# N-gram sums in 256 columns, the byte product in exact bf16 parts, y copied to SBUF right after its square

## The chip, the cores and the metric

The kernel runs on one core of a Trainium2 chip. A core has five engines that each work through their own list of instructions: PE (TensorE, matmuls and transposes; its weight loads have a row of their own, PEld), DVE (VectorE), ACT (ScalarE), POOL (GpSimd) and SP (SyncE, which only issues DMAs here). They meet through semaphores alone. The metric is the device time of one execution in microseconds (us), the median of three.

## The reference

A small language-model tower over 32 sequences of 512 byte values (16,384 tokens, width H = 128):

```
tokens   enc = [byte_emb[x], mean over n = 3..8 of gate_n * ngram_emb[n][hash of n bytes] / n] @ W_enc.T + b_enc
x3       Y = retention(layernorm(X)) + X                  4 heads of 32, decay mask, causal
         X = gelu(layernorm(Y) @ w1 + b1) @ w2 + b2 + Y
         retention: Q, K (rotated), V; A = Q K^T * decay; y = A V; y normed per head (gn_w, gn_b); swish(G) * yn @ WO
experts  add enc to X, layernorm, logits over 8 experts, top 1, two-layer FFN of that expert, added to the row
```

An n-gram that would reach past the end of its sequence adds nothing. Inputs and outputs are float32.

## The kernel before, in words

`tower_program` (line 133) writes one program per engine. Sequences are taken in 16 **pairs** (`it`); a pair has two sets `s` = 0, 1 (one sequence each) and each set two halves `h` = 0, 1 of 256 tokens (two chunks of 128). So four **streams** (s, h) run side by side, each with two PSUM banks, `bank_a` and `bank_b`. Short names below: s0h1 l1 is set 0, half 1, layer 1.

Every engine's list is made by `main_program` (line 414). Each stream has a main sequence, `attend` then `feed` for three layers (29.8 and 14.4 units), beside it `embed` of the next pair and `route` of the last, and on POOL the gathers. The pieces are generators that `yield` a number, their place in units after the piece's start; `by_progress` (line 385) always takes the piece with the lowest number next. The streams start 0, 11.91, 28.43 and 40.35 units apart (`LAGS`). So hand-written numbers set the order, engine by engine, and it is fixed when the program is built. An engine that reaches an instruction whose semaphore is not there yet stands still, with all that is behind it.

The pieces that matter, each with its semaphore waits:

- `attend`, PE (1164 to 1237): `norm_T` (two transposes of `xn`), projections q, k, v, g (1171), transposes of the rotated q and k (1182), `kv` (1189), scores (1194), values y into `bank_a` (1205), the mean squares (1218, "ms": `sq` times the head matrix into the upper half of `bank_a`), the transposes of the spread rstd into `bank_b` (1224, `rT_y`), and the output projection (1233, "o", tile `zp`).
- The same on ACT (679 to 710): copy and scale of x (`norm_T`), V and tanh of g (685, 686), copies of q, k (689, 691), square of y (696, `sq`), **spread** (701, one rstd per head written over 32 columns, tile `xn<-gr`), and copy of the transposed rstd from PSUM, scaled by `gn_w` (706, tile `zp`).
- On DVE (935 to 989): `xn` (889), rotation (949, 950, 953), swish (957, `sw`), state mask and sum (963, 969), score masks (974), eps onto the mean squares (979, `ms`), **z** (983, 984: y times scaled rstd, plus `gn_b`, times swish; it waits for 706), residual (988).
- On POOL: power -0.5 of the mean squares (611, tile `gr`) and of the norms (584, 599).
- `embed`: 12 gathers of 128 table rows on POOL (573); on DVE the one-hot of the bytes (911) and the weighted sum of the six tables, chunk by chunk (922, 926); on PE two transposes, then per chunk `side_T` times `enc_gram` and `onehot` times `pemb`, all float32 (1159 to 1162); then a norm with moments (894, 897), rstd on POOL in two instructions (590, 591) and the apply (903).
- `route`: the same norm on the last layer's output, small copies into `row` (1013 to 1017), logits, choice, places, and a scatter to DRAM.

After the pairs comes the expert phase (from 2256 us on), which the change leaves alone.

The lines on which the order hangs:

```
LAGS = ((0, 11.91), (28.43, 40.35))
...
            while min(at) < DONE:
                n = at.index(min(at))
                at[n] = next(streams[n], DONE)
...
                yield (24.26, 23.57, 21.54)[l]
                n = CH * HEADS // 2
                act.wait_ge(y_r[s], nth(k, 2, h))
```

Of the kernel before, what the change touches and what calls it, by code (L numbers as in the profile page):

```python
# [8 lines left out]
BF16 = mybir.dt.bfloat16  # L35
# [24 lines left out]
LAGS = ((0, 11.91), (28.43, 40.35))  # L60
TILE = 512
# [12 lines left out]
def columns(widths):  # L74
# [10 lines left out]
    ("before", P), ("gram_scale", NG), ("gram_valid", NG), ("vocab", 1), ("token", CH), ("rank", E),  # L85
# [10 lines left out]
def constants(n_tokens):  # L96
# [24 lines left out]
    c[:, CONST["gram_valid"]] = [[(CH - 1) * P + p + n <= S for n in GRAMS] for p in i]  # L121
    c[:, CONST["gram_row"]] = [k * HASHES for k in range(NG)]
    c[:, CONST["parity"]] = (i[:, None] // HD) % 2 == np.arange(2)[None, :]
    c[:, CONST["vocab"]] = i[:, None]
    c[:, CONST["token"]] = i[:, None] + np.arange(CH)[None, :] * P
# [3 lines left out]
    c[:, CONST["tile"]] = np.arange(64)  # L129
    return c  # L130

def tower_program(nc, x, gram_table, layer_w, params, consts, expert_w, out):
# [10 lines left out]
    with ExitStack() as ctx:  # L144
# [18 lines left out]
        gate = sb("gate", [P, 2, NG])  # L163
# [22 lines left out]
        onehot = two(sb, "onehot", [P, S])  # L186
# [6 lines left out]
        side_mom = two(sb, "side_mom", [P, 2, CH, 2])  # L193
        side_ve = two(sb, "side_ve", [P, CH])
        side_rstd = two(sb, "side_rstd", [P, 2, CH])
# [12 lines left out]
        qkT = two(sb, "qkT", [P, 2, 2, 2, P])  # L208
        qm = two(sb, "qm", [P, 2, HEADS, 2 * P])
        kv = two(sb, "kv", [P, CH - 1, H])  # L210
# [23 lines left out]
        token = two(sb, "token", [P, CH])  # L234
# [17 lines left out]
        mod_i = [lent(qm[0], 0, [NG, P], I32), lent(qm[0], GP, [NG, P], I32), lent(qm[1], 0, [NG, P], I32)]  # L252
        quot_i = lent(qm[1], GP, [NG, P], I32)
# [7 lines left out]
        past = lent(qm[0], 0, [tiles - SETS, E])[0:1]  # L261
        pastn = lent(qm[0], 64 * E, [tiles - SETS, E])[0:1]
# [37 lines left out]
        side_moments = halves("side_norm_moments_ready")  # L300
        side_scale = halves("side_norm_rstd_ready")
        n_ss = halves("norm_square_sums_ready")
        x_s = two(sem, "layer_output_ready")
        x0_s = two(sem, "layer_input_ready")
        x0_ss = two(sem, "layer_input_square_sums_ready")
# [18 lines left out]
        y_ms = two(sem, "y_square_sums_ready")  # L324
        y_r = two(sem, "y_rstd_ready")
        ms_p = two(sem, "y_square_sums_in_psum")
        rT_y = two(sem, "y_rstd_transposed")
        y_rb = two(sem, "y_rstd_spread")
        z_a = two(sem, "y_scale_ready")
# [5 lines left out]
        ff_p = two(sem, "ffn_out_in_psum")  # L335
# [63 lines left out]
        def early(part):  # L399

            for point in part:
                yield APART * point
# [18 lines left out]
        def side_norm(it, k):  # L421

            if k == 0:
                return 2 * it if it else 1
# [949 lines left out]
```

## Time and profile before

| | |
|---|---|
| Time, median of 3 | 2497.04 us (2496.94 to 2498.17) |
| The profiled execution: span of core 0, first to last instruction | 2495.6 us |
| What lies around the span (median less span) | 1.4 us |
| Mean granted clock of TensorE over the span | 0.982 |
| PE, DVE, ACT, POOL busy | 2263.5, 1897.7, 1571.6, 1817.0 us |
| Chain that ended last: PE, DVE, POOL | 61%, 17%, 9% |

The profiled execution is not one of the timed ones; its span is 1.4 us under the median of the timed ones. Times in the views are in us from the span's start, means in ns. "Idle before" is how long the engine had nothing to execute ahead of that instruction, with what ended it.
### The profile page before, as it was taken

How to read it: one execution, taken by the hardware profiler on the slowest of the kernel's cores; microseconds unless marked ns; L12 is line 12 of the kernel's file. 1: busy time of each engine (PE TensorE's matmuls, PEld its weight loads, DVE VectorE, ACT ScalarE, POOL GpSimd, SP SyncE). 2: the span in 40 equal slices, each digit the busy share in tenths (PEclk: the TensorE clock that was granted, in tenths of full speed). 3: DMA queues.
4: the chain of work that ended last, by engine and by line, in shares of the span. 5: the costliest groups of instructions: out<-in, count | busy, mean ns of one | idle time of the engine just before them, and what ended most of it. 6: DMA issues, size and time to landing. Idle time of an engine off the chain costs nothing.

```text
span 2495.6 us, 52521 instructions
## 1 busy us (share of the span) xinstructions
PE 2263.5 (91%) x18256; PEld 1944.6 (78%) x18256; DVE 1897.7 (76%) x6079; ACT 1571.6 (63%) x4925; POOL 1817.0 (73%) x1902
## 2 busy tenths in 40 slices
PE   0389999999999999999999999999999999987874
PEld 0268888888888888888888888888888888875653
DVE  6357888888797978788888788887879797766442
ACT  0157776777767677676767677677676767753431
POOL 4786777777777777777777777777777765345776
PEclk9889999999999999999999999999999999998997
DMA  3722131313131222222221313131311010004653
GB/s 111 278 63 84 24 110 27 111 26 109 28 106 30 71 66 72 65 71 68 68 71 28 109 26 110 28 108 28 110 26 41 26 27 29 3 9 120 168 157 99
DMA packets 107332, 181.47 MB, mean 73 GB/s; under 512 B 23748, under 2 KB 46406, under 8 KB 106960
## 3 DMA queue, kind: packets, MB, share of 16 engines
q1 hardware_dynamic: 73296, 110.87, 13.4%
q0 software_dynamic: 33792, 67.45, 10.2%
q8 instruction: 140, 2.29, 0.4%
q14 instruction: 104, 0.85, 0.1%
HBM read 89.54 MB, written 90.78 MB: 72 GB/s over the span
## 4 chain that ended last, share of the span: by engine, by line
PE 61%; DVE 17%; POOL 9%; issue 6%; ACT 5%; DMA 2%; POOLq 0%; DVEq 0%; SPq 0%
PE psum L1119 52%; PE psum L1138 6%; POOL grams L573 4%; POOL out L638 3%; DVE hid L974 3%; DVE side_n L926 3%; PE psum L1187 2%; ACT hid L724 1%; DVE qk L953 1%; DVE hid L950 1%; DVE qk L949 1%; POOL gr L611 1%; ACT squares L665 1%; ACT qm L691 1%; DVE zp L984 1%
## 5 line engine op out<-in xcount | busy, mean ns | idle before, releaser
L573 POOL DMA_INDIRECT grams<-gram_table,idx_all x768 | 785.2, 1022 | 197.8 <-issue 189.9
L1119 PE MATMUL psum<-xT,lw 128*128 128x256 f32 x1920 | 482.8, 384 | 0.7 <-ACT xT L677 0.7
L1119 PE MATMUL psum<-lw,hid 128*128 128x129 f32 x3072 | 405.7, 277 | 0.9 <-ACT hid L724 0.9
L611 POOL TENSOR_TENSOR gr<-ms,con 128x8 f32<-128x8 f32 x192 | 326.9, 1702 | 105.8 <-DVE ms L979 103.0
L1119 PEld LDWEIGHTS psum<-lw,hid 128*128 128x128 f32 x3072 | 376.9, 192 | 21.0 <-issue 15.6
L584 POOL TENSOR_TENSOR rstd<-ss,con 128x2 f32<-128x2 f32 x320 | 232.4, 729 | 189.5 <-ACT squares L665 185.3
L1119 PEld LDWEIGHTS psum<-xT,lw 128*128 128x128 f32 x1920 | 339.0, 192 | 31.4 <-ACT xT L677 0.9
L724 ACT ACTIVATE hid<-psum,par 128x256 f32<-128x256 f32 x768 | 318.2, 478 | 21.1 <-PE psum L1119 17.6
L677 ACT ACTIVATE xT<-psum,par 128x256 f32<-128x256 f32 x384 | 215.5, 562 | 126.4 <-PE psum L1138 122.7
L1119 PE MATMUL psum<-lw,xT 128*128 128x256 f32 (+1 forms) x1536 | 291.8, 333 | 2.0 <-ACT xT L677 1.5
L1138 PE MATMUL psum<-con,xn 128*128 128x128 f32 x1152 | 239.2, 290 | 43.1 <-DVE xn L889 21.4
L1119 PEld LDWEIGHTS psum<-lw,xT 128*128 128x128 f32 x1536 | 252.0, 194 | 28.7 <-ACT xT L677 6.8
L974 DVE TENSOR_TENSOR hid<-psum,con 128x512 f32<-128x512 f32 x384 | 247.8, 680 | 17.1 <-PE psum L1119 17.0
L1138 PEld LDWEIGHTS psum<-con,xn 128*128 128x128 f32 x1152 | 134.6, 144 | 120.0 <-issue 50.1
L1119 PE MATMUL psum<-qm,qkT 64*128 64x256 f32 x1536 | 215.3, 403 | 12.2 <-DVE kv L963 7.6
L949 DVE TENSOR_TENSOR qk<-psum,con 128x512 f32<-128x512 f32 x192 | 131.8, 686 | 83.1 <-PE psum L1119 82.9
L671 ACT ACTIVATE xn<-Y,rstd 128x128 f32<-128x128 f32 x384 | 132.6, 393 | 79.1 <-POOL rstd L584 77.2
L665 ACT ACTIVATE squares<-Y 128x129 f32<-128x129 f32 x384 | 115.3, 304 | 105.5 <-DVE Y L988 104.4
L926 DVE SCALAR_TENSOR_TENSOR side_n<-grams,gate,side_n 128x128 f32<-128x128 f32 x640 | 181.6, 344 | 0.0
L1119 PEld LDWEIGHTS psum<-qm,qkT 64*128 64x128 f32 x1536 | 135.8, 187 | 51.4 <-issue 23.6
L689 ACT ACTIVATE qkT<-psum 128x512 f32<-128x512 f32 x192 | 115.0, 599 | 85.0 <-PE psum L1187 84.0
L691 ACT ACTIVATE qm<-psum,con 128x256 f32<-128x256 f32 x384 | 160.9, 478 | 0.0
(187 smaller groups left out, 4822.2 us busy)
## 6 DMA issues: line engine op xcount, KB each, us to landing
routed_rows<-pad SPq DMA_DIRECT2D x265, 264.0 KB
grams<-expert_w SPq DMA_DIRECT2D x44, 321.0 KB, 3.0
grams<-gram_table,idx_all POOLq DMA_INDIRECT x768
grams<-routed_rows SPq DMA_DIRECT2D x44, 264.0 KB, 3.1
xb<-x SPq DMA_DIRECT2D x32, 256.0 KB
lw<-layer_w SPq DMA_DIRECT2D x1, 2503.5 KB, 12.1
routed_rows<-row,slot POOLq DMA_INDIRECT x128, 2.4
con<-consts SPq DMA_DIRECT2D x1, 1340.5 KB, 6.1
```

The lines of the kernel that those rows point to most:

```text
L573: pool.indirect_dma_start(grams[s][:, g, c, :], None, gram_table, bass.IndirectOffsetOnAxis(ap=idx_all[:, g, at:at + 1], axis=0))\
L584: pool.tensor_tensor(rstd[s][:, CS[h]], ss[s][:, CS[h]], const("half")[:, 0:2], ALU.pow)\
L611: pool.tensor_tensor(gr[s][:, c], ms[s][:, c], const("half")[:, 0:n], ALU.pow).then_inc(y_r[s], 1)
L665: last = act.activation(scratch[s][:, c, :], src[s][:, c, 1:], ACT.Square, scale=float(H) ** -0.5, accum_out=dst[s][:, c:c + 1])
L677: act.activation(xT[s][:, TS[h]], src[:, 0:2 * P], ACT.Identity, bias=b, scale=w).then_inc(xT_s[s][h], 1)
L691: last = act.activation(qm[s][:, h, j, :], bank_b(s, h)[:, 0:2 * P], ACT.Copy, scale=const("parity")[:, j:j + 1])
L724: last = act.activation(hid[s][:, h, 2 * m + f, :], src[:, f * 2 * P:(f + 1) * 2 * P], ACT.Gelu, bias=param("ffn_b1", l * FB + 2 * m + f))
L926: last = dve.scalar_tensor_tensor(acc[:, c, :], grams[s][:, g, c, :], w, acc[:, c, :], ALU.mult, ALU.add)
L949: dve.tensor_tensor(qk[s][:, cs, :], b.rearrange("p (c n) -> p c n", c=2), cos_v[:, cs, :], ALU.mult)
L974: dve.tensor_tensor(A[s][:, h, m], chunks((a, b)[m]), causal.unsqueeze(1).to_broadcast([P, HEADS, P]), ALU.mult).then_inc(sc_s[s], 1)
L1119: return pe.matmul(dst, lhsT, rhs, start=start, stop=stop)
L1138: last = pe.transpose(dst[:, (c % 2) * P:(c % 2 + 1) * P], src[:, c, :], eye)
```

## The change

1. **Byte product.** `pemb` (byte embedding times encoder, plus bias) is split during setup into three bf16 parts that add up to it exactly. The one-hot becomes bf16 and holds byte b in rows b and b + 64; the first two parts stand in the upper and lower 64 rows of one operand, the third in a second. Per chunk one float32 matmul becomes two bf16 matmuls.
2. **N-gram sums.** The weighted sum takes both chunks at once: six instructions of 256 columns for twelve of 128. N-grams past the end now point at a zero row added to the table (six small instructions in setup) instead of having their own weights.
3. **y.** ACT copies y, scaled by `gn_w`, out of PSUM right behind its square, and signals once for both. The spread rstd is transposed into the upper half of `bank_a`, and z reads it from there: the copy behind the transposes (706) is gone. norm 2 is transposed into `bank_a`. Three waits for `bank_b` move from `rT_y` to the third matmul of w1.
4. **Side norms.** DVE adds eps, POOL has one instruction instead of two. `route` writes moments and token number straight into `row`.
5. **Order.** The numbers move into one table, with the same row for both halves. Those of spread, z, `rT_y` and `ms` are new; the rest stay. `route` of the last pair starts 3 units later.

```
+AT = {
...
+    "dve ms": ((21.5, 20.5, 20), (21.5, 20.5, 20)),
+    "dve z": ((25.5, 24.5, 23.5), (25.5, 24.5, 23.5)),
+    "act spread": ((24, 23, 22), (24, 23, 22)),
+    "pe rT_y": ((25, 24, 23), (25, 24, 23)),
...
-                link(pool.tensor_scalar(side_ve[s][:, CS[h]], side_mom[s][:, k, CS[h], 1], EPS, 1.0, ALU.add, ALU.mult))
-                pool.tensor_tensor(side_rstd[s][:, k, CS[h]], side_ve[s][:, CS[h]], const("half")[:, 0:2], ALU.pow)\
...
+                return pool.tensor_tensor(ap, ap, const("half")[:, 0:2].unsqueeze(2), ALU.pow)
...
-                act.activation(sq[s][:, CS[h], :], chunks(bank_a(s, h))[:, 0:2, :], ACT.Square,
-                               scale=float(HD) ** -0.5).then_inc(y_sq[s], 1)
-                yield (24.26, 23.57, 21.54)[l]
+                act.activation(sq[s][:, CS[h], :], chunks(bank_a(s, h))[:, 0:2, :], ACT.Square)
+                act.activation(zp[s][:, TS[h]], bank_a(s, h)[:, 0:2 * P], ACT.Copy, scale=param("gn_w", l))\
+                   .then_inc(y_sq[s], 1)
+                yield at("act spread", h, l)
...
-                yield (26.38, 25.13, 23.43)[l]
-                act.wait_ge(rT_y[s], nth(k, 2, h))
-                act.activation(zp[s][:, TS[h]], bank_b(s, h)[:, 0:2 * P], ACT.Copy,
-                               scale=param("gn_w", l)).then_inc(z_a[s], 1)
...
+            for k, n in enumerate(GRAMS):
+                ends = hv[:, k, P - n + 1:]
+                last = dve.tensor_scalar(ends, ends, const("beyond"), None, ALU.max)
...
+                for n in range(3):
+                    link(dve.tensor_copy(pemb_part[:, n, :], rest))
+                    if n < 2:
+                        link(dve.tensor_tensor(pemb_rest[:, :], rest, pemb_part[:, n, :], ALU.subtract))
...
+                last.then_inc(s_hash_f, 1)
...
-                    for i, c in enumerate(half_chunks(h)):
-                        w = gate[:, (0, 0, 0, 1)[c], g:g + 1]
...
+                        dve.wait_ge(acc_step[s][h], nth(it, NG, g - 1))
+                        last = dve.scalar_tensor_tensor(acc, grams[s][:, g, CS[h], :], gate[:, g:g + 1], acc,
+                                                        ALU.mult, ALU.add)
...
-                yield (26.94, 26.44, 24.57)[l]
-                dve.wait_ge(z_a[s], nth(k, 2, h))
-                link(dve.tensor_tensor(zp[s][:, ts], a[:, 0:2 * P], zp[s][:, ts], ALU.mult))
+                yield at("dve z", h, l)
+                dve.wait_ge(rT_y[s], nth(k, 2, h))
+                link(dve.tensor_tensor(zp[s][:, ts], a[:, 2 * P:], zp[s][:, ts], ALU.mult))
...
-                    mm(bank_b(s, h)[:, chunk(c % 2)], side_T[s][:, chunk(c)], param("enc_gram"), True, False)
-                    last = mm(bank_b(s, h)[:, chunk(c % 2)], onehot[s][:, chunk(c)], pemb[:, :], False, True)
+                    mm(bank_b(s, h)[:, chunk(c % 2)], side_T[s][:, chunk(c)], param("enc_gram"), c % 2 == 0, False)
+                for c in half_chunks(h):
+                    for n in range(2):
+                        last = mm(bank_b(s, h)[:, chunk(c % 2)], onehot[s][:, chunk(c)], pemb_bf[:, n, :], False, n * (c % 2) == 1)
...
-                half_transposes(b, xn[s], h).then_inc(rT_y[s], 1)
+                half_transposes(a[:, 2 * P:], xn[s], h).then_inc(rT_y[s], 1)
...
-                norm_T(it, s, 2 * l + 1, h, b)
+                norm_T(it, s, 2 * l + 1, h, a)
```

**What it moves: PE.** In the loop over the pairs PE's order is that of before, but for the embed groups. One of them, of before (`side_T` is the transposed n-gram sum):

```order
L1138 MATMUL psum<-con,side_n0 128x128 x2
L1119 MATMUL psum<-par,side_T0 128x128
L1119 MATMUL psum<-pemb,onehot0 128x128
L1119 MATMUL psum<-par,side_T0 128x128
L1119 MATMUL psum<-pemb,onehot0 128x128
L1138 MATMUL psum<-con,xn0 128x128 x2
```

and of the change:

```order
L1192 MATMUL psum<-con,side_n0 128x128 x2
L1172 MATMUL psum<-par,side_T0 128x128 x2
L1172 MATMUL psum<-pemb_bf,onehot0 128x128 x4
L1192 MATMUL psum<-con,xn0 128x128 x2
L1172 MATMUL psum<-con,sq1 128x4 x2
```

Two float32 products with the one-hot became four bf16 ones; nothing else moved.

**ACT, place A**, layer 0 of stream s0h0: its spread (`xn0<-gr0`) against the copies of q and k of s0h1 (`qkT0`, `qm0`). Before:

```order
L665 ACTIVATE squares0_1,ss01<-X01 128x129 x2
L724 ACTIVATE hid1<-psum,par 128x256 x4
L735 ACTIVATE side_T0<-psum 128x256
L689 ACTIVATE qkT0<-psum 128x512
L691 ACTIVATE qm0<-psum,con 128x256 x2
L701 ACTIVATE xn0<-gr0 128x256
L665 ACTIVATE squares1,ss1<-Y11 128x129 x2
L706 ACTIVATE zp0<-psum,par 128x256
```

Changed:

```order
L730 ACTIVATE sq0<-psum 128x256
L731 ACTIVATE zp0<-psum,par 128x256
L699 ACTIVATE squares0_1,ss01<-X01 128x129 x2
L755 ACTIVATE hid1<-psum,par 128x256 x4
L766 ACTIVATE side_T0<-psum 128x256
L736 ACTIVATE xn0<-gr0 128x256
L723 ACTIVATE qkT0<-psum 128x512
L725 ACTIVATE qm0<-psum,con 128x256 x2
L699 ACTIVATE squares1,ss1<-Y11 128x129 x2
```

The spread now stands ahead of the copies of q and k of the other half, and y's copy behind its square.

**DVE, place C**, layer 0 of stream s1h1: its z (`zp1`) against the n-gram sum and the swish (`sw0`) of s0h1 layer 1. Before:

```order
L953 TENSOR_TENSOR qk0<-qk0,hid0 128x512
L979 TENSOR_SCALAR ms0<-psum 128x8
L926 SCALAR_TENSOR_TENSOR side_n0<-grams0,gate,side_n0 128x128 x4
L957 SCALAR_TENSOR_TENSOR sw0<-tg0,psum 128x256
L983 TENSOR_TENSOR zp1<-psum,zp1 128x256
L984 SCALAR_TENSOR_TENSOR zp1<-zp1,par,sw1 128x256
L926 SCALAR_TENSOR_TENSOR side_n0<-grams0,gate,side_n0 128x128 x4
L963 TENSOR_TENSOR kv0<-psum,con 128x128
```

Changed:

```order
L1008 TENSOR_TENSOR qk0<-qk0,hid0 128x512
L1034 TENSOR_SCALAR ms0<-psum 128x8
L1038 TENSOR_TENSOR zp1<-psum,zp1 128x256
L1039 SCALAR_TENSOR_TENSOR zp1<-zp1,par,sw1 128x256
L980 SCALAR_TENSOR_TENSOR side_n0<-grams0,gate,side_n0 128x256 x2
L1012 SCALAR_TENSOR_TENSOR sw0<-tg0,psum 128x256
L980 SCALAR_TENSOR_TENSOR side_n0<-grams0,gate,side_n0 128x256 x2
L1018 TENSOR_TENSOR kv0<-psum,con 128x128
```

z moved ahead of a piece of the n-gram sum and of the swish.

## Rows read from the trace of the kernel before

**Rows 1.** The page: busy time, share of the span and instructions of each engine.
```profile
PE 2263.5 (91%) x18256; PEld 1944.6 (78%) x18256; DVE 1897.7 (76%) x6079; ACT 1571.6 (63%) x4925; POOL 1817.0 (73%) x1902
```

**Rows 2.** 500 us of the pairs: busy PE, PEld, DVE, ACT, POOL; granted clock, DMA.
```profile
1000.00:1500.00 500.00, 490.83 (x4112) 427.71 (x4108) 411.61 (x1318) 351.70 (x1138) 389.29 (x411) 1.00 0.21 63
```

**Rows 3.** Timeline of PE: start, length, line, operation, tiles; idle in brackets.
```profile
1186.08 0.50 PE L1119 MATMUL psum<-con,sq 128*128 128x4 f32 x4
...
1202.24 0.28 PE L1119 MATMUL psum<-bias,three_bf 128*128 128x129 bf16 x2
1202.35 1.11 PE L1119 MATMUL psum<-lw,hid 128*128 128x129 f32 x8
...
1267.17 0.39 PE L1119 MATMUL psum<-pemb,onehot 128*128 128x128 f32 x2
1267.40 0.39 PE L1119 MATMUL psum<-par,side_T 128*128 128x128 f32 x2
...
1272.64 0.44 PE L1138 MATMUL psum<-con,xn 128*128 128x128 f32 x2 [0.71 <-ACT xn L701]
...
1318.08 0.50 PE L1119 MATMUL psum<-con,sq 128*128 128x4 f32 x4
```

**Rows 4.** Place A, timelines of POOL, ACT and PE.
```profile
1186.86 1.67 POOL L611 TENSOR_TENSOR gr<-ms,con 128x8 f32<-128x8 f32 x1 [0.27 <-DVE ms L979]
...
1187.33 0.60 ACT L689 ACTIVATE qkT<-psum 128x512 f32<-128x512 f32 x1
1187.82 0.83 ACT L691 ACTIVATE qm<-psum,con 128x256 f32<-128x256 f32 x2
1188.56 0.41 ACT L701 ACTIVATE xn<-gr 128x256 f32<-128x256 f32 x1
1188.88 0.29 ACT L665 ACTIVATE squares<-Y 128x129 f32<-128x129 f32 x1
...
1189.40 1.13 PE L1119 MATMUL psum<-qm,qkT 64*128 64x256 f32 x8
```

**Rows 5.** Place B, timelines of ACT, DVE and PE.
```profile
1215.26 0.42 ACT L701 ACTIVATE xn<-gr 128x256 f32<-128x256 f32 x1 [0.48 <-POOL gr L611]
...
1216.85 0.42 DVE L957 SCALAR_TENSOR_TENSOR sw<-tg,psum 128x256 f32<-128x256 f32 x1
...
1217.78 0.61 PE L1119 MATMUL psum<-V,qk 128*128 128x128 f32 x4
```

**Rows 6.** Place C, timelines of DVE and PE.
```profile
1228.45 1.13 DVE L926 SCALAR_TENSOR_TENSOR side_n<-grams,gate,side_n 128x128 f32<-128x128 f32 x4
1229.50 0.42 DVE L957 SCALAR_TENSOR_TENSOR sw<-tg,psum 128x256 f32<-128x256 f32 x1
1229.83 0.42 DVE L983 TENSOR_TENSOR zp<-psum,zp 128x256 f32<-128x256 f32 x1
...
1230.69 1.13 DVE L926 SCALAR_TENSOR_TENSOR side_n<-grams,gate,side_n 128x128 f32<-128x128 f32 x4
...
1228.86 0.38 PE L1138 MATMUL psum<-con,xn 128*128 128x128 f32 x2
...
1229.97 0.49 PE L1119 MATMUL psum<-V,qk 128*128 128x128 f32 x2 [0.29 <-DVE sw L957]
```

**Rows 7.** The square and its product, s0h1 layer 1: timelines of ACT and PE.
```profile
1236.33 0.38 ACT L696 ACTIVATE sq<-psum 128x256 f32<-128x256 f32 x1
1236.67 0.56 ACT L677 ACTIVATE xT<-psum,par 128x256 f32<-128x256 f32 x1
...
1236.83 0.59 PE L1119 MATMUL psum<-con,sq 128*128 128x4 f32 x4
```

**Rows 8.** Groups of instructions: line, form, count, busy us, mean ns, idle before.
```profile
L706 ACT ACTIVATE zp<-psum,par 128x256 f32<-128x256 f32 x192 | 92.9, 484 | 26.4 <-PE psum L1138 25.9
...
L926 DVE SCALAR_TENSOR_TENSOR side_n<-grams,gate,side_n 128x128 f32<-128x128 f32 x640 | 181.6, 344 | 0.0
L984 DVE SCALAR_TENSOR_TENSOR zp<-zp,par,sw 128x256 f32<-128x256 f32 x192 | 93.6, 487 | 6.8
```

More of the change, by code:

```diff
@@ L60 @@
 LAGS = ((0, 11.91), (28.43, 40.35))
+EARLY = ((0, 11.91), (28.43, 40.35))
+CLOSING = ((3, 3), (3, 3))
+AT = {
[4 rows of a table added]
+    "act qkT": ((12.27, 11.97, 8.14), (12.27, 11.97, 8.14)),
[8 rows of a table added]
+    "dve rope": ((7.38, 8.39, 6.59), (7.38, 8.39, 6.59)),
[6 rows of a table added]
+    "act spread": ((24, 23, 22), (24, 23, 22)),
+    "pe rT_y": ((25, 24, 23), (25, 24, 23)),
+    "pool gr": ((24.36, 21.76, 21.39), (24.36, 21.76, 21.39)),
+    "pool rstd0": ((53.27,), (53.27,)),
+    "pool rstd": ((68.34,), (68.34,)),
+    "pool rstd_r": ((10.35,), (10.35,)),
[14 rows of a table added]
+    "pool scatter": ((98.01,), (98.01,)),
+    "act accT": ((28.58,), (28.58,)),
+    "act h0": ((46.4,), (46.4,)),
+    "act ss0": ((62.88,), (62.88,)),
+    "act rT": ((23.06,), (23.06,)),
+    "dve onehot": ((2.41,), (2.41,)),
+    "dve acc2": ((4.2,), (4.2,)),
+    "dve acc4": ((5.88,), (5.88,)),
+    "dve mom0": ((49.55,), (49.55,)),
+    "dve x0": ((61.11,), (61.11,)),
+    "dve row": ((2.67,), (2.67,)),
+    "dve rn": ((11.47,), (11.47,)),
+    "dve pick": ((47.84,), (47.84,)),
+    "dve slot": ((61.5,), (61.5,)),
+    "pe accT": ((27.45,), (27.45,)),
+    "pe h0": ((40.24,), (40.24,)),
+    "pe rT": ((21.23,), (21.23,)),
+    "pe logits": ((46.06,), (46.06,)),
+    "pe places": ((59.62,), (59.62,)),
+}
 TILE = 512
@@ L335, in tower_program @@
         ff_p = two(sem, "ffn_out_in_psum")
+        r_mom = two(sem, "router_moments_ready")
+        r_scale = two(sem, "router_rstd_ready")
         r_n = two(sem, "router_norm_applied")
@@ L397, in sequences, with early @@
                     yield feed(it, s, l, h), FEED
-        def early(part):
+        def early(part, after=0):
             for point in part:
-                yield APART * point
+                yield after + APART * point
         def beside(s, h, embed, route):
-            yield early(embed(0, s, h)), FIRST + ROUTE
+            yield early(embed(0, s, h)), FIRST + ROUTE + LAGS[s][h] - EARLY[s][h]
             for it in range(pairs):
@@ L411, in beside @@
                 else:
-                    yield early(route(it, s, h)), 0
+                    yield early(route(it, s, h), CLOSING[s][h]), 0
         def main_program(embed, attend, feed, route, *others):
@@ L417, in main_program, with at @@
             by_progress(*[one_by_one(lag + FIRST, *sequences(s, h, attend, feed)) for s, h, lag in streams],
-                        *[one_by_one(lag, *beside(s, h, embed, route)) for s, h, lag in streams],
-                        *[one_by_one(lag, *other(s, h)) for s, h, lag in streams for other in others])
-        def side_norm(it, k):
-            if k == 0:
-                return 2 * it if it else 1
-            return (2 * it + 3 if it + 1 < pairs else 2 * it + 2)
+                        *[one_by_one(EARLY[s][h], *beside(s, h, embed, route)) for s, h, _ in streams],
+                        *[one_by_one(EARLY[s][h], *other(s, h)) for s, h, _ in streams for other in others])
+        def at(name, h, l=0):
+            return AT[name][h][l]
         def pads_done(group):
@@ L1000, in route @@
                 cs = CS[h]
-                yield 2.67
+                moments = row[s][:, :, H + 1:H + 3]
+                yield at("dve row", h)
                 if it:
@@ L1004, in route @@
                 dve.wait_ge(x_s[s], nth(it * LAYERS + LAYERS - 1, 2, h))
+                token = row[s][:, cs, H:H + 1].bitcast(I32)
+                dve.tensor_scalar(token, token, float(2 * S), None, ALU.add)
                 for c in half_chunks(h):
```

262 lines of the change are left out of this document (135 added, 127 removed), and 30 rows, old and new, of the table AT.

## The prediction

> **What bounds it now.** I read the page first. PE is busy 91% of the span, the others 63 to 76% [rows 1]. Then the busy time by stretch: in 500 us of the pairs PE works 490.8 us at the full granted clock (1.00, the 2.4 GHz level), DVE 411.6, POOL 389.3 and ACT 351.7 [rows 2]. So PE's list is the clockwork of the kernel. But "busy" hides small stops: a product that comes 0.1 us late is covered in this view by the modelled tail of the one before it. So I went on to the timeline, and it repeats. The product with the squares of s0h0 layer 0 starts at 1186.08 and at 1318.08 us [rows 3], which makes a **period** of 132.0 us for a pair. The 16 pairs are one start and some 15 such periods. Whatever the change does in one period counts 15 times. I made the sum for one period, against this execution (span 2495.6), and add the result to the median, which is 1.4 us more.
>
> PE stops in a period only where its next piece waits for a chain over other engines. The longest such stop with its own idle entry is the transposes of the spread rstd of s1h1 layer 1, 0.71 us after ACT [rows 3]. Another is `kv` of s0h1 layer 1, which waits for the swish on DVE [rows 6]. Everything else fits with a few tenths to spare, and the order numbers make it fit. The question for a change like this is less what it saves than which instruction comes to stand in front of which.
>
> **Part 1, the byte product: minus 0.9 us a period.** A float32 product with the one-hot takes 0.23 us (1267.17 to 1267.40) [rows 3], for two instructions. Two bf16 products of 129 columns take 0.11 us (1202.24 to 1202.35) [rows 3]. A group of two chunks goes from 2 x 0.23 to 4 x 0.055 = 0.22 us, saves 0.23 to 0.24, and a period has four groups: 0.92 us, over 64 groups **14.7 us**. The measured pair is of the same kind (weights of 128 columns in bf16, product behind product), so I take its price. The Trainium skill (TensorE: Matmul & The Clock Gate, Back-to-back issue gap) speaks against that: it gives about 81 ns for a sustained matmul of 128 columns with its weight load. By that page a group would save 0.46 - 0.32 = 0.14 us, 9 us in all. The trace does not agree for a pair of such products (55 ns each), and it has no four in a row.
>
> Not all of it is kept. Two of the four groups stand between the start of a chain and a stop that waits for it: the group at 1267 lies ahead of the 0.71 us stop at 1272.64 [rows 3]. There PE only comes earlier to the same wait. I keep half, **0.45 us**; bounds 0 and 0.92.
>
> **Part 2, sums of 256 columns: DVE 0 to -1.5 us a period, PE -0.2.** The 128-column step costs 0.284 us (181.6 us over 640) [rows 8]. A 256-column one lasts 0.487 (z's second) [rows 8] and now waits for its predecessor, some 0.035 us more (6.8 us idle over 192). Two steps at 0.57 become one at 0.52: 0.05 us on five steps and four groups, 1 us of DVE. With the larger first step I say 1.5. Side norms and `route` trade small instructions of DVE about evenly, and POOL loses eight short ones in a period. DVE's other 80% hides this. Where a PE stop waits for DVE's queue it helps by a tenth or two: I take 0.2 us for all.
>
> **Part 3, y copied early.** The copy costs ACT 0.484 us before and after [rows 8]; the removed step was copy, plus two semaphore hops, between `rT_y` and z. So z may start some 0.5 us earlier. Before that, the squares' product now waits for square and copy. At s0h1 layer 1 the square starts at 1236.33, ACT could take the copy at 1236.67, it ends 0.48 later at 1237.15, and the product, which started 0.12 us after the square's end, starts at 1237.27 instead of 1236.83 [rows 7]: plus 0.44. There are twelve such places in a period, so the bounds are 0 and 5.3 us. Most have slack; I expect four to be touched, three of them partly hidden by a stop that follows or by a chain that z's earlier start shortens. I take **0.3 us**, near the one place that is sure. The moved waits for `bank_b` cost nothing: what they wait for was done microseconds before, and they now come later.
>
> **Part 4, the order.** This decides. On PE nothing moved, but ACT and DVE execute what comes next or stand still.
>
> *Place A, +0.9 us.* POOL's power for s0h0 ends at 1186.86 + 1.67 = 1188.53. Before, ACT used that time for the q and k copies of s0h1 (1187.33 to 1188.65) and did the spread at 1188.56. Now the spread stands ahead of them. It can't start sooner, so ACT waits 1.2 us, and the copies start at 1188.56 + 0.32 = 1188.88 and end 1.32 us later, 1190.20. PE's scores of s0h1 started at 1189.40 [rows 4]. They need these copies, so they start at 1190.3: 0.9 us late. Behind them on PE stand the second half of w2 of s1h0 and all the rest. The bounds are 0.8, if a wake-up costs nothing, and 1.0.
>
> *Place B, +0.4 us.* The same for s1h0 layer 0. The spread, which waits for POOL until 1215.26 in either order, now has q and k of s1h1 behind it, and V and tanh of s0h0 behind those; V moves from 1215.58 to 1215.26 + 0.32 + 1.23 = 1216.8. Tanh ends at 1217.5, and z (0.86 us, see C) also has been put ahead of the swish on DVE. The swish goes from 1216.85 to 1217.7 and ends at 1218.1; `kv` on PE stood at 1217.78 [rows 5] and starts at 1218.2.
>
> *Place C, +1.3 us.* z of s1h1 layer 0 stood behind a piece of the n-gram sum and the swish of s0h1. It now stands ahead of both, at 1228.45. But its transposes run on PE at 1228.86 and end at 1229.24, and their place on PE is the same. DVE idles 0.8 us, does z (0.86 us, from 1229.83 to 1230.69), then the piece of the sum (1.05 us before, 1.0 now), and comes to the swish at 1229.28 + 0.86 + 1.0 = 1231.1 instead of 1229.50. `kv` of s0h1 already waited for the swish at 1229.97 [rows 6], so all of it reaches PE: +1.6 us. The scores behind it had waited some 0.3 us for DVE, which is now covered: 1.3 net. Bounds: 1.0 and 1.6.
>
> *Elsewhere*: z of s0h1 layer 1 stands ahead of a rotation, an `ms` of layer 2 behind a piece of the sum, and z of s0h0 layer 2 ahead of a residual. Each moves a chain by 0.7 to 1 us (one z, 0.86 us, or one piece of the sum, 1.05) [rows 6] that has some slack. I take **0.5 us** for all; the bounds are 0 and 2.6, three times z.
>
> **The sum of a period**: 0.9 + 0.4 + 1.3 + 0.5 + 0.3 - 0.45 - 0.2 = 2.75 us. These were worked out one by one, while a stop early in the period gives the later chains slack. So I take 0.4 off: **2.35 us**, 15 times **35 us**. The start adds, as an estimate, 1 us for six small instructions ahead of the gather indices (a tenth or two each, well under the 0.41 us of a 256-column step [rows 6]) and 1.5 for place A, where ACT waits for a POOL busy with gathers; the end, a single chain, gains about 1 by z's shorter path and the lighter norms. In all +36: 2497 + 36 = **2533 us**. A measurement can tell about 0.2% (5 us) from no change.
>
> **The rivals.** *PE's work is what counts* (faster): PE is 98% busy in the pairs [rows 2], so what is taken from it comes off the end and the new waits fall into slack. For it: PE's share, and z's chain is 0.5 us shorter. The Trainium skill says so as well (Perfetto Trace Analysis, Identifying Performance Opportunities: improve the most-contended engine). Against it: places A and C, where an engine is made to wait for something that cannot be there. It gives -14.7, 2482 us. Chance 0.13.
>
> *Only the early copy costs* (same): the order works out, but the squares' product waits 0.44 us at two places in a period: +13 us against -14.7. 2495 us, chance 0.07.
>
> *Every wait adds up* (slower still): nothing is absorbed, the saving is all lost at the stops. Then the sum is 3.4, and with twice the allowance for the places elsewhere 3.9 us, +58 or so: 2558 us. Chance 0.12.
>
> *The forecast*: chance 0.68. Its own range is 1.2 to 3.5 us a period, 2515 to 2550. That the queues hold strictly is its condition. The skill says they do (TensorE: Matmul & The Clock Gate, the table at its head: strict FIFO on ACT, DVE and POOL). ACT's 0.48 us of idle ahead of the spread, with V of another half ready behind it [rows 5], agrees.
>
> **Range and chances.** From 2502, which leaves out the two quick cases, to 2555, which takes in most of the slow one. Faster 0.13, same 0.07, slower 0.80.
>
> **What would show it.** In the profile after: a period of 134 to 135 us; four bf16 products in 0.22 us in the embed groups; DVE idle some 0.8 us ahead of the z of s1h1 layer 0, released by PE; ACT idle over 1 us ahead of the spread of s0h0 layer 0, with the q and k copies behind it; more idle on PE for ACT's q and k copies and for the swish. PE's share should fall to about 89%. I am wrong if the period is 131 to 132 us, or if it is longer while ACT and DVE never wait at A and C.

## The result, and the profile after

| | before | changed |
|---|---|---|
| Time, median of 4 runs each | 2496.99 us (2496.45 to 2498.17) | 2575.97 us (2573.95 to 2577.18) |
| Ratio | | 1.0315, 95% interval 1.0300 to 1.0329 |
| Span of the profiled execution | 2495.6 us | 2574.3 us |

Slower by 79 us. The forecast was plus 36 (2533 us), its range ended at 2555 and the slowest rival stood at 2558. The sign was right, the size less than half.

The page of the changed kernel, busy time of each engine, for [rows 1]; then 500 us of the pairs, for [rows 2]:

```profile
PE 2284.7 (89%) x18258; PEld 1942.4 (75%) x18258; DVE 1880.7 (73%) x5582; ACT 1555.8 (60%) x4925; POOL 1767.6 (69%) x1774
```

```profile
1000.00:1500.00 500.00, 478.55 (x3974) 412.91 (x3973) 396.62 (x1169) 337.55 (x1104) 365.03 (x367) 1.00 0.21 67
```

In 500 us every engine is busy for less time: PE 478.6 us for 490.8. No engine became fuller; what grew is the time in which they wait for each other. The chain that ended last was 61% PE before, and is now:

```profile
PE 47%; DVE 22%; POOL 15%; issue 9%; ACT 6%; DMA 1%; POOLq 0%; SPq 0%; DVEq 0%
```

PE's timeline over one period, changed kernel, for [rows 3] to [rows 7] (read in short windows, so that a group can show fewer products than it has):

```profile
1173.62 0.39 PE L1172 MATMUL psum<-pemb_bf,onehot 128*128 128x128 bf16 x4
1173.84 0.39 PE L1192 MATMUL psum<-con,xn 128*128 128x128 f32 x2
...
1224.35 0.39 PE L1172 MATMUL psum<-con,sq 128*128 128x4 f32 x3
...
1228.73 0.49 PE L1172 MATMUL psum<-qm,qkT 64*128 64x256 f32 x2 [0.78 <-ACT qm L725]
...
1257.75 0.49 PE L1172 MATMUL psum<-V,qk 128*128 128x128 f32 x2 [0.23 <-DVE sw L1012]
...
1271.61 0.49 PE L1172 MATMUL psum<-V,qk 128*128 128x128 f32 x2 [1.85 <-DVE sw L1012]
...
1279.08 0.38 PE L1172 MATMUL psum<-con,sq 128*128 128x4 f32 x2 [0.67 <-ACT zp L731]
...
1287.73 0.44 PE L1243 MATMUL psum<-con,qk 128*128 128x128 f32 x2 [0.23 <-DVE qk L1008]
...
1315.34 0.33 PE L1243 MATMUL psum<-con,qk 128*128 128x128 f32 x1 [0.36 <-DVE qk L1008]
...
1360.42 0.39 PE L1172 MATMUL psum<-con,sq 128*128 128x4 f32 x3
```

From one product with the squares of s0h0 layer 0 to the next it is 136.07 us, for 132.0. Each named place has its row: A at 1228.73, B at 1257.75, C at 1271.61, the early copy at 1279.08. The idle entry is a little under what PE loses, since the modelled tail of the last product covers some 0.2 us. Measured from start to start against the same pieces without a wait, A went from 0.15 to 1.00 us, B from 0 to 0.39, the `kv` of C from 0.45 to 2.01.

What the queues look like there, first ACT at place A, then DVE at place C:

```profile
1227.04 0.41 ACT L736 ACTIVATE xn<-gr 128x256 f32<-128x256 f32 x1 [1.38 <-POOL gr L645]
1227.36 0.58 ACT L723 ACTIVATE qkT<-psum 128x512 f32<-128x512 f32 x1
```

```profile
1269.36 0.42 DVE L1038 TENSOR_TENSOR zp<-psum,zp 128x256 f32<-128x256 f32 x1 [0.89 <-PE psum L1192]
1269.82 0.48 DVE L1039 SCALAR_TENSOR_TENSOR zp<-zp,par,sw 128x256 f32<-128x256 f32 x1
1270.22 1.00 DVE L980 SCALAR_TENSOR_TENSOR side_n<-grams,gate,side_n 128x256 f32<-128x256 f32 x2
1271.14 0.41 DVE L1012 SCALAR_TENSOR_TENSOR sw<-tg,psum 128x256 f32<-128x256 f32 x1
```

ACT stands 1.38 us for POOL with the q and k copies ready behind it. DVE stands 0.89 us for the transposes, then does z and the sum piece, and the swish on which PE waits comes last. Both are as the prediction drew them.

The view of waits sums such idle time over the whole span (engine, line, what it waited for: us, times, longest). Of PE's rows the ones that bear on the change, before and then changed:

```profile
PE psum L1138 <- ACT xn L701: 18.5, 33, 2.5
PE psum L1119 <- ACT qm L691: 3.3, 7, 1.2
PE psum L1119 <- DVE sw L957: 3.1, 11, 0.3
PE psum L1119 <- ACT sq L696: 1.8, 3, 0.8
```

```profile
PE psum L1172 <- DVE sw L1012: 32.4, 32, 1.9
PE psum L1172 <- ACT zp L731: 15.6, 33, 1.1
PE psum L1172 <- ACT qm L725: 13.4, 17, 1.2
PE psum L1192 <- ACT xn L736: 12.6, 25, 2.5
PE psum L1243 <- DVE qk L1008: 7.4, 26, 0.6
```

Larger rows, such as one wait of 37.0 us before and 38.0 now, lie in the main in setup and the expert phase and differ by at most 3.4 us.

Two things the prediction did not have. The swish and the square with its copy now stand first among the waits of the pairs, the second with 33 waits, two in a period. And the periods are not alike: of the fourteen behind the first (from the first projection of s0h0 in one pair to that in the next), nine are 135.7 to 136.1 us and five 137.4 to 138.0. In those five TensorE's clock falls right behind place C. Windows of 3.4 us (columns as in [rows 2], the granted clock third from the end), four of the five, and the same place in an ordinary period:

```profile
724.70:728.10 3.40, 3.40 (x18) 2.98 (x18) 1.38 (x5) 0.51 (x2) 0.68 (x1) 0.50 0.19 43
997.80:1001.20 3.40, 3.40 (x16) 3.08 (x15) 1.12 (x4) 0.81 (x3) 0.96 (x1) 0.50 0.14 39
1543.90:1547.30 3.40, 3.40 (x18) 3.07 (x17) 1.12 (x4) 0.81 (x3) 0.96 (x1) 0.50 0.17 43
1953.50:1956.90 3.40, 3.40 (x18) 3.07 (x18) 1.14 (x5) 0.70 (x2) 0.95 (x1) 0.50 0.15 39
1271.90:1275.30 3.40, 3.40 (x29) 2.86 (x29) 2.60 (x8) 1.01 (x4) 0.96 (x1) 1.00 0.13 39
```

At 0.50, the 1.2 GHz level, PE gets 16 to 18 instructions through where 29 fit at 1.00. It was full in all of them; what came before was the stop of 1.85 us, which ended 0.2 to 0.6 us before the clock fell. That stop is as long in the nine periods where the clock stays. The kernel before has no such stretch between 160 and 2230 us.

### The profile page after: what moved, and what is told of

It reads as the page before. It is cut to its first block, busy times and chain, and to the rows that moved or that the text cites. A ratio compares the mean times of both kernels' runs of the same rounds, so it can differ in the third digit from the quotient of the medians.

```text
span 2574.3 us, 51781 instructions
## 1 busy us (share of the span) xinstructions
PE 2284.7 (89%) x18258; PEld 1942.4 (75%) x18258; DVE 1880.7 (73%) x5582; ACT 1555.8 (60%) x4925; POOL 1767.6 (69%) x1774
## 4 chain that ended last, share of the span: by engine, by line
PE 47%; DVE 22%; POOL 15%; issue 9%; ACT 6%; DMA 1%; POOLq 0%; SPq 0%; DVEq 0%
PE psum L1172 41%; POOL grams L610 5%; PE psum L1192 4%; POOL out L672 3%; DVE hid L1029 3%; POOL gr L645 3%; DVE qk L1008 2%; POOL rstd L621 2%; ACT squares L699 2%; DVE qk L1004 2%; DVE hid L1005 2%; PE psum L1243 2%; DVE zp L1039 2%; DVE zp L1038 2%; DVE side_n L980 2%
## 5 line engine op out<-in xcount | busy, mean ns | idle before, releaser
L610 POOL DMA_INDIRECT grams<-gram_table,idx_all x768 | 769.8, 1002 | 198.9 <-issue 190.1
L1172 PE MATMUL psum<-qm,qkT 64*128 64x256 f32 x1536 | 216.1, 404 | 21.6 <-ACT qm L725 13.4
L736 ACT ACTIVATE xn<-gr 128x256 f32<-128x256 f32 x192 | 81.0, 422 | 158.5 <-POOL gr L645 158.1
```

The costliest lines, as they stand in the source:

```text
L610: pool.indirect_dma_start(grams[s][:, g, c, :], None, gram_table, bass.IndirectOffsetOnAxis(ap=idx_all[:, g, at:at + 1], axis=0))\
L1172: return pe.matmul(dst, lhsT, rhs, start=start, stop=stop)
```

## The experiments

The theory after the comparison: the new order numbers cost most (places A, B, C and waits behind them, and the clock behind C). The rival: the early copy holds up the squares' product and all else follows.

**One set of four, the kernel before at 2496.5 us beside them.** First the order numbers of before on the otherwise changed kernel:

```diff
-    "dve ms": ((21.5, 20.5, 20), ...      "dve z": ((25.5, 24.5, 23.5), ...
+    "dve ms": ((21.32, 21.92, 19.52), ... "dve z": ((26.94, 26.44, 24.57), ...
-    "act spread": ((24, 23, 22), ...      "pe rT_y": ((25, 24, 23), ...
+    "act spread": ((24.26, 23.57, 21.54), ... "pe rT_y": ((25.36, 23.79, 22.97), ...
```

> The change with the four order rows of the kernel before (ms, z, spread, transposes of the rstd); everything else of the change stays, the early copy of y too. Theory 1, the order: places A, B and C cost 0.85 + 0.39 + 1.34 = 2.6 us a period by the stops of PE in the two traces, two waits for the copies of q and k another 0.9, and the stretches at half clock some 9 us in all; 15 x 3.5 + 9 = 61 us go, 2515 us are left. Theory 2, the early copy is what costs (the product with the squares waits, and all else follows from the late chain): then 30 us or more stay above the kernel before, 2540 us or more. In both the squares' product still waits, 1.4 us a period.

Measured 2502.09 us, ratio to before 1.0022 (1.0012 to 1.0031). Undoing the order numbers takes back 74 of the 79 us. The rival is out. The estimate of 61 was too small: an ordinary period got 3.9 us shorter and not 3.5, mainly because the squares' product of s0h1 layer 1 now waits 0.3 us where it waited 0.8; the first pair gave 5.4 us, and the end 3.8, which the estimate did not have.

Then z's number alone:

```diff
-    "dve z": ((25.5, 24.5, 23.5), (25.5, 24.5, 23.5)),
+    "dve z": ((26.94, 26.44, 24.57), (26.94, 26.44, 24.57)),
```

> The change with z's order row alone put back. Theory 1: place C goes (1.34 us a period net), a wait for the rotated q and k with it (0.4), and every stretch at half clock in the middle of the pairs (some 9 us), while A and B stay: 2576 - 15 x 1.75 - 9 = 2541 us. Rival, the early copy holds z's chain back anyway: z is late wherever it stands, less than 15 us go, 2561 us or more. Rival on the clock: it falls for another reason than the stop at place C, then the half-clock stretches stay and 2550 is left.

Measured 2527.89 us, ratio 1.0129 (1.0112 to 1.0146): 48 us for z. And place B is gone: `kv` of s0h0 layer 1 follows its predecessor without a stop, although the spread still stands ahead of V. The waits for the q and k copies grew instead:

```profile
PE psum L1172 <- ACT qm L725: 29.7, 33, 1.2
PE psum L1192 <- ACT xn L736: 10.4, 22, 1.7
PE psum L1172 <- ACT zp L731: 7.7, 33, 0.9
```

29.7 us for 13.4, and 33 times for 17: once the swish is no longer late, the scores of s0h1 layer 1 wait for the copies that stand behind the spread. Place C had hidden that.

Then the old y path on top of the old numbers: the square signals by itself, the copy waits for the transposes in the other bank.

```diff
-                act.activation(zp[s][:, TS[h]], bank_a(s, h)[:, 0:2 * P], ACT.Copy, scale=param("gn_w", l))\
-                   .then_inc(y_sq[s], 1)
...
+                yield (26.38, 25.13, 23.43)[l]
+                act.wait_ge(rT_y[s], nth(k, 2, h))
+                act.activation(zp[s][:, TS[h]], bank_b(s, h)[:, 0:2 * P], ACT.Copy, scale=param("gn_w", l))\
+                   .then_inc(z_a[s], 1)
```

> As e1_old_numbers, and also part 3 undone: the square signals by itself, y's scaled rstd is copied behind the transposes, which go to the other bank again. What is left of the change is the bf16 byte product, the 256-column sums and the lighter norms. Theory 1 and the prediction's terms: 0.65 us a period under the kernel before, 2487 us; the difference to e1_old_numbers is then the true price of the early copy, 28 us, where the waits of the squares' product alone would make 1.4 x 15 = 21 and the prediction's term 5. Rival, the early copy pays for itself by z's shorter chain: within 8 us of e1_old_numbers.

Measured 2488.61 us, ratio 0.9968 (0.9957 to 0.9978). The early copy, with the move between banks that goes with it, costs 13.5 us under the old order, 0.9 a period. It lies between the two figures expected, and well above the prediction's 0.3. The row of s0h1 layer 1 with the early copy and old order, and without it:

```profile
1239.20 0.61 PE L1172 MATMUL psum<-con,sq 128*128 128x4 f32 x4 [0.15 <-ACT zp L731]
```

```profile
1229.34 0.59 PE L1175 MATMUL psum<-con,sq 128*128 128x4 f32 x4
```

Last the kernel before with the bf16 byte product and nothing else:

```diff
-                    last = mm(bank_b(s, h)[:, chunk(c % 2)], onehot[s][:, chunk(c)], pemb[:, :], False, True)
+                for c in half_chunks(h):
+                    for n in range(2):
+                        last = mm(bank_b(s, h)[:, chunk(c % 2)], onehot[s][:, chunk(c)], pemb_bf[:, n, :], False, n * (c % 2) == 1)
```

> The kernel before with the byte product in bf16 parts and nothing else. Prediction: half of 0.92 us a period is kept, 2490 us. Rival, PE's work is what counts: 14.7 us, 2482 us. Rival, nothing is kept since the stops behind take it all: 2497 us. If four bf16 products in a row cost 81 ns each and not 55, a group saves 0.14 us and the whole 9 at the most: 2488 us or more, and the starts of the products in the trace are 0.32 us apart over a group instead of 0.22.

Measured 2488.76 us, ratio 0.9971 (0.9959 to 0.9984): 7.7 us, half of the 14.7. Its trace has the four in a row, 0.23 us from start to start of what follows:

```profile
1131.45 0.39 PE L1137 MATMUL psum<-pemb_bf,onehot 128*128 128x128 bf16 x4
1131.68 0.39 PE L1157 MATMUL psum<-con,xn 128*128 128x128 f32 x2
```

The stop at s1h1 layer 1, ACT's spread ahead of the transposes, has the size it had (0.96 us from start to start in both; `ACT xn` costs PE 18.9 us in it, for 18.5 before). Had the group ahead of it only brought PE sooner to the same wait, it would be 0.23 us longer, so the other half does not go there. The traces have it at other places: 0.12 us at the squares' product of s1h1 layer 1, 0.18 at the transposes right ahead of that of s0h1 layer 2, which wait for `xn` of DVE, and 0.05 at each of two more products.

**A second set of four, before at 2496.4 us.** z's number for place C alone:

```diff
-    "dve z": ((25.5, 24.5, 23.5), (25.5, 24.5, 23.5)),
+    "dve z": ((25.5, 24.5, 23.5), (26.94, 24.5, 23.5)),
```

> The change with z's order number of layer 0 put back for the second halves (h = 1) alone: place C, where z stands ahead of a piece of the n-gram sum and of the swish, and one spot in s0h1. Theory 1, with the stop of 1.85 us that makes the clock fall: 1.3 us a period and the 3.4 us stretches at half clock among the pairs go (9 us), 2576 - 20 - 9 = 2547 us. Rival on the clock: the stretches come from PE's idle share as a whole and stay, 2556 us. Rival on the place: z of layers 1 and 2 carries most of the 48 us that z's three numbers brought, then 2560 us or more are left.

Measured 2541.08 us, ratio 1.0179 (1.0162 to 1.0196). One entry of the table is worth 35 us. The clock is 1.00 from 160 to 2230 us, with no stretch below, where the changed kernel has 0.99. This kernel, then the changed one:

```profile
160.00:2230.00 2070.00, 1995.68 (x16597) 1723.67 (x16600) 1645.53 (x4837) 1414.15 (x4612) 1468.13 (x1476) 1.00 0.19 58
```

```profile
160.00:2230.00 2070.00, 1976.31 (x16321) 1704.99 (x16322) 1623.38 (x4760) 1389.91 (x4534) 1458.98 (x1465) 0.99 0.19 58
```

The period is 134.6 us, 1.4 less than an ordinary one of the change: from start to start `kv` of s0h1 loses 1.8 us less and the squares' product behind it 0.5 less, but the scores 1.1 more, for the q and k copies. The slow periods that are gone bring 8.5 us, the first pair 5.9.

The spread's numbers alone:

```diff
-    "act spread": ((24, 23, 22), (24, 23, 22)),
+    "act spread": ((24.26, 23.57, 21.54), (24.26, 23.57, 21.54)),
```

> The change with the spread's three order numbers put back (ACT's order but for the y copies as before): places A and B go (0.85 + 0.39), and the wait for q and k of s0h1 layer 2 that stayed with z's old numbers (0.5); the stop ahead of the transposes of s1h1 layer 1 comes back (0.5). Theory 1: 2576 - 15 x 1.2 = 2557 us. Rival: place C holds the period anyway, and what is won at A and B is lost there: within 5 us of the change.

Measured 2558.43 us, ratio 1.0250 (1.0232 to 1.0267), 17.5 us. PE's timeline at A, B and C, and at s0h1 layer 2:

```profile
1218.33 1.13 PE L1172 MATMUL psum<-qm,qkT 64*128 64x256 f32 x8
...
1247.36 0.71 PE L1172 MATMUL psum<-V,qk 128*128 128x128 f32 x4 [0.23 <-DVE sw L1012]
...
1261.21 0.49 PE L1172 MATMUL psum<-V,qk 128*128 128x128 f32 x2 [1.85 <-DVE sw L1012]
...
1305.69 0.44 PE L1192 MATMUL psum<-con,xn 128*128 128x128 f32 x2 [0.71 <-ACT xn L736]
1305.96 0.60 PE L1243 MATMUL psum<-con,qk 128*128 128x128 f32 x4
```

A is gone. **B is not**: with ACT's order as before it is as large as ever, so it is z ahead of the swish that makes it, not the spread. The wait at 1315.34 of the change is gone too, and the 0.71 us stop of before is back. C is there, and with it the stretches at 0.50, in six of the fourteen periods here. With z's new number the spread's costs 17.5 us; with z's old one it costs, together with `ms` and `rT_y`, 2527.9 - 2502.1 = 26 us, since C no longer hides the late q and k copies.

The number of `ms` alone:

> The change with the order numbers of ms (eps onto the mean squares) alone put back. Theory 1: it moves one small instruction of DVE in s1 layer 1 and layer 2, worth a few tenths at the most, 2570 to 2577 us. Rival: the late ms of layer 1, behind z, is part of the chain that ends in the wait for the rotated q and k, then 6 us or more go.

Measured 2576.86 us, ratio 1.0323 (1.0305 to 1.0340): nothing. The ordinary period grew to 136.5 us and there were two slow ones for five, although PE stops 1.92 us at C in every period.

A version that might keep z's shorter chain and lose the stop: y is copied right behind the spread, while PE transposes the spread into the other bank.

```diff
                    .then_inc(y_rb[s], 1)
+                act.activation(zp[s][:, TS[h]], bank_a(s, h)[:, 0:2 * P], ACT.Copy, scale=param("gn_w", l))\
+                   .then_inc(z_a[s], 1)
```

> As e5_old_y (order and banks of before, light norms, 256-column sums, bf16 product), but y is copied on ACT right behind the spread, while PE transposes the spread into the other bank; the square signals by itself. Keeps z's shorter chain without the wait of the squares' product. Expected if the mechanism is right: no stop at the squares' product, those at the output projection gone, 2484 us (2480 to 2488) against 2488.6. Rival: 0.48 us of copy behind the spread comes ahead of V, tanh or the q and k copies of another stream and costs at each of two or three such places what it takes there: 2495 us or more.

Measured 2488.65 us, ratio 0.9969 (0.9957 to 0.9982), the same as with the old y path. The shorter chain of z brings nothing under the old order, where 2484 us was expected: the stops that end with z are few there, and the copy behind the spread makes the scores of s0h1 layer 1 wait 0.3 us longer for the q and k copies (0.92 us from start to start for 0.61), which was the rival. Both beat the kernel before by 0.3%, and both leave out of the change what cost.

**Sets that say less.** The next ten runs came on chips where the kernel before took 2635, 2634 and 2596 us. There engines stop for 2 us and more with no releaser in the trace (shown as "remote"), as in these rows of the waits of e14_spread_s1h1 (DVE, then ACT), which no trace of the two sets above has:

```profile
DVE X L1055 <- remote: 29.5, 15, 2.2
```

```profile
ACT xT L712 <- remote: 33.7, 14, 3.3
```

Only ratios within a set can be read. Place C by itself, on the old numbers:

```diff
-    "dve z": ((26.94, 26.44, 24.57), (26.94, 26.44, 24.57)),
+    "dve z": ((26.94, 26.44, 24.57), (25.8, 26.44, 24.57)),
```

> As e1_old_numbers, with place C alone made as in the change: z of s1h1 layer 0 behind the ms and ahead of the piece of the n-gram sum and the swish. The prediction's term, 1.3 us a period, 20 us, gives 2522 us; if the stop of PE is again 1.85 us and the clock falls behind it in a third of the periods, 8 us more, 2530 us. Rival on the clock: it falls only with the change's other stops as well, 2522 us and no stretch at half clock among the pairs. Rival on additivity: with z's other places as before the period absorbs half of it, 2512 us.

> The kernel of e15_place_c_alone a third time. Where the kernel before takes 2497 us: 2522 us by the prediction's 1.3 us a period, 2530 us with the clock falling behind the stop in a third of the periods, 2512 us if half is absorbed. Where it takes 2635 us again: 21 us above it, as in the two sets so far.

It ran three times, in one set of each chip (e15_place_c_alone, r15_place_c, q15_place_c): 2658.85, 2655.67 and 2618.34 us, ratios 1.0073 (1.0045 to 1.0100), 1.0082 (1.0065 to 1.0099) and 1.0087 (1.0061 to 1.0114). With 1.0022 for the same kernel without it, C alone costs 0.5 to 0.65%, 13 to 16 us, if the ratios carry over; the prediction's term would be 20. The traces say more. PE stops 1.80 to 1.85 us at C in nearly every period of all three, and the scores behind it come 0.35 us sooner than without the edit: some 1.45 us a period at the place itself, 22 us in all, with A, B and the rest as in the old order. Whether the period absorbs the rest of it or the other stops of these chips cover it stays open. In q15_place_c the clock falls behind C in three of the fourteen periods and nowhere else among them, so the change's other stops are not needed for that.

The early copy in the new order, copied behind the spread instead:

> The change with all its new order numbers, but y is copied behind the spread instead of behind the square, the square signals by itself, and the transposes of the rstd go to the other bank. Theory: the stops of the squares' product (1.4 us a period in the change) are the copy's alone and go, 2576 - 20 = 2556 us. Rival: half of them are a late y by the new order (in e9_old_spread one of them moved from 0.79 to 0.60 us with nothing but ACT's order), then 2564 us. Second rival: with the spread ahead of V and of the q and k copies, 0.48 us of copy behind it costs there what it frees, within 5 us of the change.

> The kernel of e12_copy_behind_new_order a third time. Where the kernel before takes 2497 us: 2556 us if the stops of the squares' product are the copy's alone, 2564 us if half of them are the new order's, 2571 us or more if the copy behind the spread costs what it frees. Where it takes 2635 us again: 63 us above it.

Three times as well (e12_copy_behind_new_order, r12_copy_behind, q12_copy_behind), 2698.86, 2696.55 and 2673.6 us, ratios 1.0245 (1.0213 to 1.0277), 1.0247 (1.0220 to 1.0274) and 1.0294 (1.0270 to 1.0318); the change stood at 1.0315 elsewhere. Between 5 and 17 us better, and not settled. The traces show what is gained and lost. Two of the change's three stops of the squares' product (s0h1 layer 0, s1h1 layer 1) are gone; at s0h1 layer 1 some 0.3 to 0.4 us of 0.81 stay without any copy ahead, so that part is the new order's. The scores at place A start 0.36 us later than in the change, since the copy now stands ahead of those of q and k.

Place A alone:

> The change with the spread's order number of layer 0 put back for the first halves alone: place A, and the spread's part of place B. The prediction's term for A: 0.85 us a period at the scores of s0h1 layer 0 go, 13 us, and with place C's 1.85 us stop still there the half-clock stretches stay: 2563 us. In e9_old_spread the stop of place B stayed with the spread's old numbers, so the spread has no part in it and nothing more is expected here. Rival: place C is fed by the same chain and takes back what A gives, 2572 us or more.

Twice (e13_spread_one_place, r13_spread), 2680.5 and 2674.79 us, ratios 1.0156 (1.0129 to 1.0184) and 1.0142 (1.0124 to 1.0159), 40 us better than the change on the other chips where 13 were expected. The changed kernel itself did not run on these chips, so this isn't a price of place A. In both traces the scores of s0h1 layer 0 start 0.20 us behind their predecessor, for 1.05 in the change, and the stop at C is still 1.8 us: C took nothing back.

The one order number of the change that helps (the spread of s1h1 layer 1 ahead of V):

> As e5_old_y, with one order number moved by 0.13: the spread of s1h1 layer 1 stands ahead of V and tanh of s0h1, where the power of POOL is ready 0.3 us after V began. What may be better than both kernels: the 0.85 us stop ahead of the transposes shrinks to the 0.27 that it has in the change, 0.58 us a period, 2488.6 - 9 = 2480 us. Rival: PE comes earlier to the next wait, or V and tanh 0.6 us later make one, 2486 us or more.

Twice (e14_spread_s1h1, r14_spread_s1h1), 2633.44 and 2628.5 us, ratios 0.9990 (0.9971 to 1.0008) and 0.9985 (0.9970 to 1.0000): no gain over the 0.9968 of the kernel that it was built on can be seen. The stop did shrink in e14_spread_s1h1, from 0.85 to a mean of 0.34 us from start to start; `kv` of s0h1 layer 1, behind the later V and tanh, lost 0.83 us for a mean of 0.10 in e5_old_y, as the rival had it, though part of that may be the chip's.

Not tried: the square signalling by itself while the copy stays right behind it. PE would write the bank that ACT reads, and what that does no run here shows.

## Why the prediction was wrong, and where it was right

The forecast was plus 36 us and the kernel got 79 slower. Its signs held: PE's share fell to 89%, DVE stood 0.89 us ahead of z, ACT 1.38 ahead of the spread. The period was to be 134 to 135 us and was 136.07.

**Part 1, right in both numbers, wrong in where the half goes.** 0.055 us for a bf16 product, also with four in a row. By the Trainium skill's 81 ns (TensorE: Matmul & The Clock Gate, Back-to-back issue gap) a group would last 0.32 us; it lasts 0.22 to 0.23, so the trace disagrees. Half was kept (0.49 us a period in e6_bf16_only for 0.45), but not for the reason given: the 0.71 us stop did not take it. Taking half was luck.

**Part 2, right.** The old-path kernel has a period of 131.2 us where the bf16 product alone has 131.5: 0.2 to 0.3 us, with the lighter norms in it. The medians are equal all the same (2488.61 and 2488.76), since its end is 5.5 us longer.

**Part 3, mis-sized: 0.3 us forecast, 0.9 measured alone, some 1.4 of stops in the change.** The step that failed is "I expect four to be touched, three of them partly hidden", with its value of 0.3. Four were touched: with the old order the squares' product loses 0.24, 0.30, 0.37 and 0.23 us against e5_old_y (s0h1 layers 0 and 1, s1h1 layer 1, s0h1 layer 2), and of these 1.14 us the period shows 0.9. In the change the fourth is hidden behind another stop, and the other three lose 0.24, 0.81 and 0.37. The 0.81 are not the copy's alone, since the square itself comes later there in the new order. One sure place was taken as the value, although the sum of like places was what had to be bounded; "most have slack" was said and not read off for the other eleven.

**Place A, right**: 0.85 us for 0.9, by ACT's queue as drawn.

**Place B, right in size (0.39 for 0.4), wrong in cause.** The step gave the delay to both, V and tanh 1.2 us later behind the spread and z ahead of the swish. The spread's old numbers leave B, z's old ones take it away. V came later and had the slack.

**Place C, right for the stop, without its effect on the clock.** `kv` lost 1.56 us more, its scores 0.2 less: 1.36 net against 1.3. Not in the sum: the clock. The prediction put that at nothing, without a reason. The stop of 1.85 us was followed by 3.4 us at half clock in five periods, 8.5 us in all (137.6, 137.4, 138.0, 137.8 and 137.7 against 136.0). Without the stop (z's number back at C alone, or all of z's) there is none. On these chips the stop is needed for it and isn't enough: the same stop brought it in five of fourteen periods in the change, in six with the spread's old numbers and in two with the `ms` number.

**Elsewhere, 0.5 forecast.** The q and k transposes of s1h0 layer 1, behind a rotation that waited for z, cost 0.39 and were on the list. Those of s0h1 layer 2 cost 0.49, and weren't: that is the spread, which the prediction looked at for layer 0 alone. `ms` was on the list and costs nothing. Half a dozen of 0.1 to 0.33 us, the largest at an embed group of s1h1, are in the main paid for by two gains: the stop of 1272.64 [rows 3] lost 0.59 us less, a `places` product 0.35.

**The discount of 0.4, wrong.** The period absorbed nothing of the sum. The whole sum without it, with 1.4 for the copy, is 2.75 + 1.1 = 3.85 us a period; ordinary periods grew by 4.05. Costs hid behind one another (the late q and k copies behind C), which makes each look small when it is undone alone and the set look large: 48 (z) and 17.5 (spread) alone, 74 together, with `ms` worth nothing and the number of `rT_y` moving nothing on PE. That is the opposite of slack. One slip of arithmetic changes no verdict: the slowest rival's +58 gives 2555 us, or 2557 with start and end, and not 2558.

**Start and end.** The first pair took 6.1 us more, 2 more than an ordinary period, with 6.8 us at half clock at 168 us; the rest from the last pair's start to the last w2 8.5 us more (with 6.8 us at half clock, before 3.4), where plus 1.5 in all was forecast. In the kernel with the old order and y path that end is still 4.2 us longer than before (155.4 against 151.2 us up to the last w2), and why was not tested; `route` starts 3 units later there, and 10.2 us of the end are at half clock, for 3.4 before.

So of the 79 us: 15 x 4.05 = 61 for the ordinary period, 8.5 for the clock, 2 for the first pair, 8.5 for the end, less 0.9 at the start. Of the 43 us that the forecast lacks, some 16 are part 3, 8.5 the clock, 8 start and end, 6 the discount and 3 the other small stops. The rival of twice the allowance elsewhere (58 us) came closest, and still had neither the clock nor the end.

## What to carry to other kernels

When each engine's order is written by hand, undo the order before the arithmetic: the good part of this change, the bf16 product, gave 8 us (the wider sums nothing that a median shows), the early copy took 13.5, and the order numbers that put instructions ahead of their inputs took 74. Read the slack of every place that an edit repeats, not of the one where it is sure to hurt. And price a long stop on a busy TensorE with what its clock does next, not with its own length alone.

## What was not expected of the hardware

- A stop of 1.85 us in a TensorE that was 96% busy was followed, in two to six of fourteen periods, by 3.4 us at the 1.2 GHz level. That was worth 1.4 to 2.0 us each time in the changed kernel and 0.8 to 1.4 in the kernels with the old numbers of the spread or of `ms`. In the other periods the same stop was followed by none.
- Chips differ. The kernel before took 2496 us on two and 2596 to 2635 us on three. Instructions were as long there as elsewhere (the copy of q and k 0.60 us in both, the power on POOL 1.72 to 1.73 us for 1.70 to 1.73), and the traces show stops of an engine for which they give no releaser.
